# Roots of the norms by bit shift and Newton steps on VectorE, and one stage for the second attention's norm and projections

## The reference, cut to what matters

```python
x = L0_attn_hidden_states                                  # (2, 1024, 256) float32
x = x + _layernorm(_L0_attn_ref(_layernorm(x), ...))       # 16 heads of 128, causal, rope
x = x + _layernorm(_L0_ffn_ref(_layernorm(x), w1, w2, w3)) # ternary weights, width 704
x = x + _layernorm(_L1_attn_ref(_layernorm(x), ...))       # 32 heads of 8, 8 key/value heads
x = x + _layernorm(_L1_ffn_ref(_layernorm(x), ...))        # width 1024, silu
def _layernorm(x, axis=-1, eps=1e-05):
    m = jnp.mean(x, axis=axis, keepdims=True)
    v = jnp.var(x, axis=axis, keepdims=True)
    return (x - m) / jnp.sqrt(v + eps)
```

## Time and profile before

| what | value |
|---|---|
| time, median of 3 runs | 1792.9 us (1791.9 to 1794.68) |
| the profiled execution | 1793.79 us, of which the span of the trace is 1791.9 us |
| granted TensorE clock, mean | 0.964 |
| busy: TensorE, VectorE, ScalarE, GpSimd | 1619.5, 1362.8, 1090.8, 690.1 us |
| VectorE, ScalarE instructions | 2792, 2092 |

### The profile page before, as it was taken

One profiled execution on the slowest core, in us unless ns is written; L12 is line 12 of the kernel. 1 busy time (PEld: TensorE's weight loads), 2 busy tenths in 40 slices (PEclk: granted clock), 3 DMA queues, 4 the chain that ended last, 5 costly groups with the idle time before them and its releaser, 6 DMA issues. The chain is left out here.

```text
span 1791.9 us, 42720 instructions
## 1 busy us (share of the span) xinstructions
PE 1619.5 (90%) x14612; PEld 1011.7 (56%) x14612; DVE 1362.8 (76%) x2792; ACT 1090.8 (61%) x2092; POOL 690.1 (39%) x804
## 2 busy tenths in 40 slices
PE   3899999999999999999965848899999999986997
PEld 1577777877777877777852524333333333323555
DVE  3477877877877878878768657989898988836774
ACT  4566666666666666666645642266666666665553
POOL 1655555555545545545504126021212121224012
PEclk9899999999999999999996969899999999987999
DMA  4322111221211221211100030100000000000001
GB/s 138 93 52 49 47 41 45 49 50 45 49 41 44 50 50 44 50 41 44 41 1 1 1 109 9 19 13 16 14 15 16 14 17 12 10 1 1 1 13 36
DMA packets 53108, 61.85 MB, mean 35 GB/s; under 512 B 11345, under 2 KB 32018, under 8 KB 53010
## 3 DMA queue, kind: packets, MB, share of 16 engines
q1 hardware_dynamic: 53010, 60.55, 13.8%
HBM read 18.57 MB, written 2.10 MB: 12 GB/s over the span
## 5 line engine op out<-in xcount | busy, mean ns | idle before, releaser
L1705 ACT ACTIVATE a_prob<-psum 128x1024 f32<-128x1024 f32 (+3 forms) x384 | 290.8, 813 | 181.9 <-PE psum L1669 181.8
L1745 DVE TENSOR_REDUCE a_mx<-psum 128x1 f32<-128x512 f32 (+3 forms) x608 | 366.3, 655 | 35.7 <-PE psum L1651 23.4
L1737 POOL TENSOR_SCALAR_AFFINE_SELECT a_prob<-a_prob 128x256 f32<-128x256 f32 x256 | 102.5, 406 | 380.3 <-ACT a_prob L1705 377.6
L1648 PE MATMUL psum<-a_kd,a_qp 128*128 128x512 f16 (+3 forms) x768 | 226.3, 339 | 20.0 <-DVE a_mx L1745 6.4
L446 POOL TENSOR_TENSOR a_swp<-a_swp,a_sin 128x512 f32<-128x512 f32 x128 | 163.2, 1275 | 161.0 <-DMA a_swp<-a_lin 161.0
L802 DVE TENSOR_REDUCE a_nmax<-psum 128x1 f32<-128x1024 f32 (+7 forms) x256 | 191.0, 747 | 1.0 <-PE psum L517 1.0
L674 ACT ACTIVATE a_prob_big<-psum,a_nmax 128x1024 f32<-128x1024 f32 (+3 forms) x128 | 121.9, 952 | 103.2 <-DVE a_nmax L802 101.4
L1648 PEld LDWEIGHTS psum<-a_kd,a_qp 128*128 128x128 f16 x768 | 70.9, 98 | 194.2 <-DVE a_mx L1745 130.7
L1690 PE MATMUL psum<-a_prob,a_vg 128*32 128x512 f32 (+3 forms) x1536 | 164.5, 500 | 6.6 <-POOL a_prob L1737 5.9
L450 POOL TENSOR_TENSOR a_rope<-a_swp,a_cosd 128x512 f32<-128x512 f32 x128 | 164.0, 1281 | 12.5 <-POOL a_swp L446 4.8
L797 DVE TENSOR_TENSOR a_pt_lo_big<-psum,a_pt_hi_big 128x512 f16<-128x512 f32 (+3 forms) x256 | 138.4, 581 | 30.2 <-ACT a_pt_hi_big L669 30.2
(11 more groups left out here) (278 smaller groups left out, 4381.1 us busy)
## 6 DMA issues: line engine op xcount, KB each, us to landing
a_swp<-a_lin SPq DMA_DIRECT2D x256, 128.0 KB, 2.3
a_qp<-a_q_part SPq DMA_DIRECT2D x192, 16.0 KB
a_kd<-a_k_part SPq DMA_DIRECT2D x192, 16.0 KB
x<-_attn_hidden_states_dram SPq DMA_DIRECT2D x4, 512.0 KB, 5.7
a_w_raw<-in_L_attn_Wq_dram SPq DMA_DIRECT2D x16, 128.0 KB, 2.2
a_w_raw<-in_L_attn_Wk_dram SPq DMA_DIRECT2D x16, 128.0 KB, 2.3
a_w_raw<-in_L_attn_Wv_dram SPq DMA_DIRECT2D x16, 128.0 KB, 2.3
a_wo_raw<-in_L_attn_Wo_dram SPq DMA_DIRECT2D x1, 2048.0 KB
```

The source lines that it names most:

```text
L1648: last = pe.matmul(to[:, j * n:(j + 1) * n], qp[:, w % 3, t * P:(t + 1) * P], kd[:, w % 3, j0 + j, a:e], start=True, stop=not edge)
L1705: act.activation(prob_at(u, i)[:, 2 * pair:2 * pair + 2, a % BANK:a % BANK + e - a], c.psum[:, pair_of(u, i):pair_of(u, i) + 2, 0:e - a], ...
L1745: dve.tensor_reduce(mx[:, t, j0:j0 + per, a // BANK], work(("S", w, i))[:, 0:per * (e - a)].rearrange("p (j n) -> p j n", j=per), AX.X, AL ...
```

## The change

`root` is gone. After `variance`, `normaliser` computes 1/sqrt on VectorE: a shift of the bits and a multiply-add on them as integers (two `tensor_scalar`), then three Newton steps of three instructions each, every one waited for, and `shift`. x of the first stage is waited for piece by piece. The stages "mid2" and projections are one: transposes go through two PSUM banks, projections of a chunk start when its tokens are transposed, v is multiplied last, the loops are unrolled, and the row of -1 comes by a GpSimd memset of one partition and four transfers, in place of the VectorE additions.

Of `constants` and `Moments` (the rest of the instructions of `variance` stays; every call of `root` is taken out, in `norm_and_turn` and in `normed_ffn`):

```diff
-            sp.wait_ge(x_loaded, 64)
...
-    def root(self, act, g):
...
-        act.activation(self.sd[:, t0:t1], self.var[:, t0:t1], ACT.Sqrt).then_inc(self.sd_ready, 1)
...
     def normaliser(self, dve, g):
...
-        self.then_wait(dve, g, 6, dve.reciprocal(self.inv[:, t0:t1], self.sd[:, t0:t1]))
...
+        whole = lambda b: b[:, t0:t1].bitcast(mybir.dt.int32)
+        self.then_wait(dve, g, 7, dve.tensor_scalar(whole(self.vy), whole(self.var), 1, None, ALU.logical_shift_right))
+        self.then_wait(dve, g, 8, dve.tensor_scalar(whole(self.seed), whole(self.vy), -1, self.MAGIC, ALU.mult, ALU.add))
+        y = self.seed
+        for i in range(3):
+            self.then_wait(dve, g, 9 + 3 * i, dve.tensor_tensor(self.vy[:, t0:t1], self.var[:, t0:t1], y[:, t0:t1], ALU.mult))
+            self.then_wait(dve, g, 10 + 3 * i, dve.scalar_tensor_tensor(out=self.gap[:, t0:t1], in0=self.vy[:, t0:t1], scalar=-0.5,
+                                                                        in1=y[:, t0:t1], op0=ALU.mult, op1=ALU.mult))
+            new = self.rstd if i == 2 else self.seed
+            self.then_wait(dve, g, 11 + 3 * i, dve.scalar_tensor_tensor(out=new[:, t0:t1], in0=self.gap[:, t0:t1], scalar=1.5,
+                                                                        in1=y[:, t0:t1], op0=ALU.add, op1=ALU.mult))
+        dve.scalar_tensor_tensor(out=self.shift[:, t0:t1], in0=self.msum[:, t0:t1], scalar=-0.5, in1=self.rstd[:, t0:t1],
+                                 op0=ALU.mult, op1=ALU.mult).then_inc(self.norm_ready, 2)
```

Of the one stage in `attention_1`, SyncE's list (after the loads of wq, wk, wv, wo, cos and sin and the three loads of f1's weights) and GpSimd's:

```diff
+                    sp.wait_ge(line_made, 1)
                     sp.wait_ge(zeroed, 2)
-                    sp.wait_ge(lined, J)
+                    for j in range(J):
+                        row = j * R + 3 * HD1
+                        sp.dma_start(kd[row:row + 1, :, j, :], line_of_minus_ones).then_inc(lined, 16)
+                    sp.wait_ge(lined, 16 * J)
                     sp.wait_ge(lo_done, (CB - 1) * NJ + 2)
                     load_rows(sp, 0)
...
+                    pool.memset(line_of_minus_ones, -1.0).then_inc(line_made, 1)
                     pool.memset(kd[:, :, :, :].bitcast(F32), 0.0).then_inc(zeroed, 1)
                     pool.memset(qp[:, :, :], 0.0).then_inc(zeroed, 1)
...
+                    pool.wait_ge(lined, 16 * J)
```

```diff
+                    norm.statistics(dve, c.x, 0, TPC)
+                    norm.variance(dve, 0)
+                    norm.statistics(dve, c.x, TPC, 2 * TPC)
+                    norm.normaliser(dve, 0)
+                    dve.wait_ge(loaded, 64)
+                    weight_low(0, "q")
+                    weight_low(1, "k")
+                    norm.statistics(dve, c.x, 2 * TPC, NT)
+                    norm.variance(dve, 1)
+                    low(0)
+                    low(1)
+                    norm.normaliser(dve, 1)
+                    weight_low(2, "v")
+                    weight_low(3, "o")
+                    dve.wait_ge(consts, 32)
+                    low(2)
+                    low(3)
```

More of the change, by code:

```diff
@@ L1409, in attention_1, with pair, turn_bank @@
             NJ = len(jobs)
[L1411 to L1418, removed]
+            norm = Moments(c, "mid2", [(0, TPC), (TPC, NT)], pctx)
+            xn = psb("xn", [P, 4, 2, D])
+            xn_ready, turned, x_hi, x_lo = (sem(n) for n in ("xn_ready", "turned", "x_hi", "x_lo"))
+            def pair(m):
+                return slice(m * 2 * P, (m + 1) * 2 * P)
+            line_of_minus_ones = rope[:, :, :].bitcast(F16)[0:1, :, :]
+            line_made = sem("line_made")
+            def turn_bank(m):
+                return c.psum[:, 6 + m % 2, :].rearrange("p (k n) -> p k n", k=KT)
             with nc.Block() as block:
@@ L1437, in _ @@
                     pool.wait_ge(zeroed, 6)
-                    with pool.Fori(0, CH) as ch:
+                    pool.wait_ge(lined, 16 * J)
+                    for ch in range(CH):
                         for m, (n, tile) in enumerate(jobs):
@@ L1475, in _ @@
-                def _(pe):
-                    pe.wait_ge(wlo, 3)
+                            if ch == 0:
+                                pe.wait_ge(wswap, 4 if n == "k" else 8)
+                            wait(pe, sin_done, (ch - 1) * NJ + m + 1)
+                            for s, ww in enumerate((part, swapped)):
+                                terms = [(k, w, a) for k in range(KT) for w, a in ((0, 0), (0, 1), (1, 0))]
+                                for i, (k, w, a) in enumerate(terms):
+                                    last = pe.matmul(c.psum[0:rows, 2 * m + s, :],
+                                                     ww[n][w][:, k, tile * P:tile * P + rows],
+                                                     (c.xT_hi, c.xT_lo)[a][:, k, tok],
+                                                     start=(i == 0), stop=(i == len(terms) - 1))
@@ L1478, in _ @@
+                            last.then_inc(made, 1)
+                    for m in range(4):
+                        turn(m)
+                    chunk(0)
+                    turn(4)
+                    turn(5)
+                    chunk(1)
+                    turn(6)
+                    turn(7)
+                    chunk(2)
+                    chunk(3)
+                    pe.wait_ge(wlo, 4)
                     for t in range(NT):
```

186 lines of the change are left out of this document (96 added, 90 removed).

## The result

The changed kernel takes 1799.55 us (median of 8 runs, 1798.06 to 1803.99), the kernel before 1793.98 us in the same comparison (8 runs, 1791.9 to 1797.29): ratio 1.0033, 95% interval 1.0022 to 1.0043, so 5.6 us slower. The forecast was 1795.8, its range ended at 1799.0, and its likeliest class was no change. 1.1 us of the miss is the level of the kernel before, 1792.9 in the runs shown then and 1793.98 now; the change itself was forecast at +2.9 us and measured at +5.6.

The account below looks back on a forecast made before the run. TensorE, busy nine tenths of the span, was taken as the bound except where stages start or end. Terms -2.8 + 3.8 - 0.2 + 2.1 = +2.9 us on a 1792.9 median gave 1795.8 us, range 1788.5 to 1799.

Parts of the forecast that it names:

- Stage "in", -2.8: First stage: statistics start 5.0 us earlier on the first piece of x, two norms cost +1.45 and +0.75; sum -2.8 us.
- With the memsets: Merged second-attention stage: GpSimd memsets delay norm 0 from 6.0 to 12.8 us, taking 6.6 of 6.8 us won; -0.2.
- the forecast's 4.5 us for the first job: Merged stage: the first of twelve projection jobs, partly at TensorE's low clock, was taken as 4.5 us.
- the prediction's case without memsets: Merged stage with no memset holding VectorE: norms ready at 6.0 and 14.3 us, scan at 59.7, 6.8 us won.
- f0, +3.8: Block f0: TensorE's start, chunk 1's normaliser beside GpSimd additions and the tail lose, chunks 1 and 2 gain; sum +3.8 us.
- f1, +2.1: Block f1: +1.2 us up to TensorE's unbroken stretch and +0.95 in the tail; sum +2.1, bounds +1.2 and +3.2.
- +1.3, half of it under a wait: Start of f1: y's second normaliser adds 1.3 us, half of it hidden under a wait for the up product.
- The chunk 1 norm under additions, +0.5 net: f1, chunk 1: normaliser beside GpSimd's additions, as in f0 but from a later root, costs +0.5 us net.
- A small `tensor_scalar` does not pass the memsets: Denies the rival that small instructions pass the merged stage's memsets: 6.6 us less, 1789.2 us, chance 0.27.
- that rival's 3.5: Merged stage: TensorE stays at the low clock one and a half jobs more, +3.5 us, 1799.3; chance 0.10.
- the third rival: f0, chunks 1 and 2: table loads cost more than their row, 2 x 1.28 us more won, 1793.2; chance 0.03.
- TensorE in f1 unbroken to the last product: f1: TensorE never waits from 1661.92 to the last down product, so only the first 50 us and tail can change.

Follow-up runs that it names:

- the piecewise run: The kernel before with only the wait for x changed, so stage "in" starts its statistics on the first piece; 1787.98 us, ratio 0.9963.

## Why the prediction was wrong

The sign was right, the size was half, and three terms carry the 2.8 us between +2.9 and +5.7.

- **Stage "in", -2.8: right**, with both its parts (5.0 for x, 2.2 for the norms, from the piecewise run).
- **"With the memsets": the failed step.** It said that variance 0's L155 "waits from 1.8 to 2.7", the end of the line's memset, and that shift and multiply-add then wait for `kd` and `qp`. I took it that a waiting instruction gets in at the next change of GpSimd's instruction, as it does in f0 at the change from an addition to the next scaling. From the line to `kd` and from `kd` to `qp` it did not: one instruction waited out all three, 8.61 us. The stage's norms came 1.6 and 1.8 us later than forecast, and the scan about 1.0 (mean of four); the forecast's 4.5 us for the first job, 4.6 and 3.4 us in the two profiles of the changed kernel, can make up for part of the norms' delay. With waits put in, the forecast came true; with the form changed, the prediction's case without memsets came true. So the rule (`tensor_scalar` held, two-input steps free) and the rest of the stage's sum were right, the hand-over was not. One slip in the sum: 12.8 - 6.0 is 6.8, not 6.6, so by its own figures this term is 0.0 rather than -0.2.
- **f0, +3.8, measured +4.6: right in kind, mis-sized.** TensorE's start +2.5 (2.4), `product` of tile 1 +1.7 (1.5), scaling +4.6 (4 to 4.2), chunks 1 and 2 -0.8 each as forecast, tail +1.35 at the last scaling (1.15). The stretched steps took 4.03 us from the bit shift to the end of `shift` (3.9 forecast), but `hidden_low` ahead of them was stretched to 1.00 as well, which I had not counted. After these the shift stands at +3.0 and at the last down copy at +3.4 (2.7 forecast); the 0.3 in between are unexplained.
- **f1, +2.1, measured +3.1: mis-sized in one term.** First y norm 0.0 (-0.1), first x norm +0.8 (+0.7), tail +1.05 (0.95). The first product comes 0.9 later, so nothing of y's second normaliser ("+1.3, half of it under a wait") shows there. "The chunk 1 norm under additions, +0.5 net" was the error: tile 1's product comes 1.3 us earlier than before, and then the norm, from shift to scaling, takes 4.77 us where 1.37 had stood, so the scaling is +2.1. The steps averaged 0.37 and the last, 0.72, was held for a whole addition on the path to ScalarE. Holding the additions back brought it to 2.4. The sum "+1.2" was also not the sum of its terms: -0.1, 0.7, half of 1.3 and 0.5 are 1.75.
- **The rivals.** A small `tensor_scalar` does not pass the memsets. The clock moved this stage by 1.2 us between two profiles of the same kernel; that is a third of that rival's 3.5, and nothing shows that the change made it worse. The 21 loads that went gave nothing beyond the chains' own length: chunks 1 and 2 of f0 gained the forecast 0.8 us each, not 1.3 or 1.4 more. The drain that the third rival counts is not seen in f1 of the kernel before: a copy on ScalarE ends at 1771.63, the table load runs from 1771.65 to 1772.93 and the Sqrt starts at 1772.94.
- **TensorE in f1 unbroken to the last product: right.** Its stretch took 10.50 us for the 36 matmuls that took 9.45 before, after a pause of 6.6 instead of 3.2 us; but the stretch from there to the last down copy is 118.9 to 120.3 us in kernels with the old root there and 119.1 to 120.1 with the new one, so no term follows from it.

Still open is what decides whether a waiting `tensor_scalar` gets in at a change of GpSimd's instruction. It did not from the line to `kd` and from `kd` to `qp` in any profile with the memsets in this place and form, and did from `qp` to `vg` and from addition to scaling; the size of the memset that follows, its element type and its layout all differ between these, and no run varied one of them alone. Nor did a run try how short a pause is enough.

## What to carry to other kernels

Before moving a chain of small VectorE instructions beside GpSimd work, look at each instruction's form and at what GpSimd issues: a `tensor_scalar` can wait out a whole row of memsets. A second operand or later memsets took the hold away; waits between the memsets only shortened it, by 1.7 us at the norm. In this kernel ScalarE's root was worth its table loads wherever the chain behind it was waited for; take the loads away only where they, and not the chain, are on the path. Price each place by itself: read by stages, the three parts of this change (the wait for x, the merged stage, the root) were each worth -5.0, -2.4 and +12.6 us to the kernel before.

## What the runs showed of the hardware

- A `tensor_scalar` on 128 x 4 elements lasted 8.61 us (8.60 with the old root) beside memsets of 2.65, 5.21 and 2.65 us. The Trainium skill (page "SBUF — State Buffer", section "Who interferes with whom") says that VectorE in a two-port mode, which `tensor_scalar` can enter, contends with GpSimd, and that whoever issues first has the shared pair for the whole instruction; the runs agree, and add that the first turn can pass from one memset to the next, though it doesn't at every change of instruction. The int32 shift and multiply-add are held like the float32 form (3.69 and 2.68 us).
- Statistics (`bn_stats`, one input, 128 x 256 elements a tile, four tiles) took 1.41 us inside the memset of `kd`, the same as in stage "in".
- Two-input steps on 128 x 4 and 128 x 12 elements take 0.15 to 0.17 us inside the same memsets, and up to 0.72 us beside additions of 0.55 to 0.73 us, which read SBUF. By that section of the Trainium skill two inputs collide with a GpSimd instruction that reads, not with one that only writes; the trace agrees.
- The granted clock in the 20 us around and after the same scaling was 0.82 in one profile and 0.88 in another of one kernel, and the second attention's length, whose code never changed, 487.2 to 490.2 us.
